# Attention and expert kernel on one core: TensorE's steps in a new order, grouped by the shape in which the array is tiled

## What is computed

```python
h = _layernorm(x) * (1 + ca) + sa
x = x + ga * attn(h)      # 16 heads of 64, 4 key/value heads, window 128, soft cap 30
h = _layernorm(x) * (1 + cb) + sb
x = x + gb * moe(h)       # 8 experts, top 1, capacity 512 tokens, relu MLP 128-512-128
# attn: scores = 30 * tanh(q.k / (8 * 30)), softmax over the last 128 tokens, times v, times Wo
```

## Time and profile before

| what | value |
| --- | --- |
| median of 3 runs | 445.53 us |
| the profiled execution, first to last instruction | 445.2 us |
| mean granted TensorE clock, share of full | 0.984 |
| TensorE busy | 425.6 us (96%) |
| VectorE, ScalarE, GpSimd busy | 295.0, 301.1, 310.4 us |
| share of TensorE in the chain that ended last | 89% |

### The profile page before, as it was taken

How to read it: one execution, slowest core, us unless ns; L and a number is a source line. 1 busy time by engine, 2 the same in 40 slices (tenths; PEclk the granted TensorE clock), 3 DMA queues, 4 the chain that set the end, 5 groups by cost and what they waited for, 6 DMA issues and landing times.

```text
span 445.2 us, 15084 instructions
## 1 busy us (share of the span) xinstructions
PE 425.6 (96%) x5662; PEld 296.0 (66%) x5662; DVE 295.0 (66%) x884; ACT 301.1 (68%) x541; POOL 310.4 (70%) x496
## 2 busy tenths in 40 slices
PE   7989999999999999999999999999998988999992
PEld 3856666665767676667676766667674554789992
DVE  6466476866776767666868585767667666386751
ACT  4887676868786868687868687867765634555540
POOL 3545666778886878687878776777687784266563
PEclk8899999999999999999999999999999998999998
DMA  8654702010111111011112210212121044595110
GB/s 240 215 175 161 215 3 84 27 32 22 52 39 38 33 55 58 20 47 52 57 41 72 64 33 20 77 40 61 37 69 43 27 143 125 186 367 198 35 44 28
DMA packets 33023, 37.15 MB, mean 83 GB/s; under 512 B 3650, under 2 KB 29255, under 8 KB 32952
## 3 DMA queue, kind: packets, MB, share of 16 engines
q1 hardware_dynamic: 29448, 27.43, 19.9%
q0 software_dynamic: 3072, 8.37, 5.2%
q10 hardware_dynamic: 432, 0.40, 0.4%
HBM read 15.69 MB, written 16.91 MB: 73 GB/s over the span
## 4 chain that ended last, share of the span: by engine, by line
PE 89%; DVE 4%; issue 2%; POOL 2%; DMA 1%; ACT 1%; POOLq 0%; SPq 0%; DVEq 0%; ACTq 0%
PE turns L504 13%; PE own L468 8%; PE turns L392 8%; PE turns L524 7%; PE turns L511 6%; PE turns L472 6%; PE turns L798 6%; PE turns L394 6%; PE turns L393 6%; PE turns L538 4%; PE turns L543 3%; PE turns L539 3%; PE own L461 2%; PE own L736 2%; PE turns L550 1%
## 5 line engine op out<-in xcount | busy, mean ns | idle before, releaser
L1189 DVE COPY_PREDICATED own<-before,turns 128x1024 f32<-128x1024 uint32 x56 | 68.8, 1228 | 41.7 <-PE turns L472 41.7
L1707 POOL TENSOR_TENSOR OL<-O,OH 128x512 fp32r<-128x512 f32 x64 | 81.7, 1284 | 16.3 <-ACT OH L923 16.2
L910 ACT ACTIVATE PR<-own 128x1024 f32<-128x1024 f32 x64 | 65.4, 1022 | 15.6 <-DVE own L1189 15.6
L1698 POOL TENSOR_SCALAR_AFFINE_SELECT PM<-PR 128x1024 f32<-128x1024 f32 x64 | 70.2, 1098 | 7.4 <-ACT PR L916 7.1
L916 ACT ACTIVATE PR<-PR 128x1024 f32<-128x1024 f32 x64 | 67.2, 1050 | 0.1
L468 PE MATMUL own<-Q,K 64*32 64x128 f32 (+3 forms) x896 | 58.7, 441 | 2.8 <-issue 1.4
L472 PE MATMUL turns<-Q,K 64*32 64x128 f32 (+3 forms) x896 | 57.4, 429 | 0.0
L1222 DVE TENSOR_TENSOR O<-turns,R 128x512 f32<-128x512 f32 x64 | 43.0, 682 | 18.3 <-PE turns L511 18.2
L1752 POOL DMA_INDIRECT sorted_rows<-PAY,slot_i x32 | 34.6, 1080 | 14.9 <-issue 10.7
L472 PEld LDWEIGHTS turns<-Q,K 64*32 64x32 f32 x896 | 36.6, 107 | 9.5
L896 ACT ACTIVATE Q<-turns 128x512 f32<-128x512 f32 x64 | 38.3, 600 | 6.6 <-PE turns L394 5.4
(11 more groups left out here) (207 smaller groups left out, 1065.8 us busy)
## 6 DMA issues: line engine op xcount, KB each, us to landing
sorted_rows<-empty_row SPq DMA_DIRECT2D x8, 776.0 KB, 6.0
VM<-V SPq DMA_DIRECT2D x56, 64.0 KB, 2.1
out_dram<-PAY SPq DMA_DIRECT2D x32, 64.0 KB, 2.4
w_stage<-w_dram SPq DMA_DIRECT2D x8, 256.0 KB
PR<-sorted_rows SPq DMA_DIRECT2D x2, 776.0 KB, 9.3
x_sb<-sorted_rows SPq DMA_DIRECT2D x2, 776.0 KB, 11.6
x_sb<-x_dram SPq DMA_DIRECT2D x3, 512.0 KB, 5.8
O<-w_dram SPq DMA_DIRECT2D x4, 256.0 KB, 4.0
```

The costliest lines, as they stand in the source:

```text
L910: act.activation(pr, own[:, :, :].rearrange("p a n -> p (a n)"), ACT.Tanh, scale=SCORE_SCALE).then_inc(tanhed, 1)
L1189: dve.copy_predicated(own[:, :, :].rearrange("p a (r n) -> p (a r) n", n=P), before[:, :].bitcast(U32).unsqueeze(1).to_broadcast([P, 2 * R ...
L1698: pool.affine_select(out=PM[:, u % P_RING, :].rearrange("p (r n) -> p r n", n=P), in_=PR[:, u % P_RING, :].rearrange("p (r n) -> p r n", n ...
L1707: pool.tensor_tensor(OL[:, t % 2, :, half], O[:, t % 2, :, half], OH[:, t % 2, :, half].bitcast(F32), ALU.subtract).then_inc(ol_done, 1)
```

## The change

The work of TensorE is the same 391 steps. What changes:

- The order. `sums(t)` now stands right before `attend(t)` (both begin at 128*32), and the first half of the next score right after it (corrections and scores are both 64*32). The projections of a block stand together. The same count gives 160 changes of form: 52 from the whole array to a tiled form, 52 back, 56 between tiled forms; 22 of them lie before `score(4, 1)` and 18 from `score(30, 0)` on. 25 times a 128*32 step follows another, 23 times a 64*32 step another; before, this happened once.
- In `attend`, the waits for the masked probabilities and for VD move from its head to its corrections.
- New banks for nearly every step, with a longer table of exceptions for the first and last tiles.
- New orders on ScalarE, VectorE and GpSimd, with longer prologues and epilogues written out. The order of SyncE is the same, and so is all from the expert stage on.

```diff
 OF_TILES = ("before", "pv", "sums", "y", "h2", "logits", "count")
 HOME = {
-    ("idle",): 5, ("columns",): 4, ("rows",): 2,
-    ("before", 0, 0): 3, ("before", 0, 1): 1, ("before", 1, 0): 0, ("before", 1, 1): 3,
-    ("count", 0): 2, ("count", 1): 0,
-    ("h2", 0): 2, ("h2", 1): 1,
-    ("k",): 1,
-    ("logits", 0): 3, ("logits", 1): 2,
-    ("pv", 0): 1, ("pv", 1): 3,
-    ("q", 0): 3, ("q", 1): 5, ("q", 2): 5, ("q", 3): 2,
-    ("sums", 0): 1, ("sums", 1): 5,
-    ("v",): 4,
-    ("wo",): 4,
-    ("x",): 0,
-    ("y", 0): 0, ("y", 1): 5,
+    ("columns",): 4,
+    ("idle",): 5,
+    ("rows",): 2,
+    ("before", 0, 0): 0, ("before", 0, 1): 0, ("before", 1, 0): 1, ("before", 1, 1): 0,
+    ("count", 0): 4, ("count", 1): 4,
+    ("h2", 0): 4, ("h2", 1): 4,
+    ("k",): 2,
+    ("logits", 0): 2, ("logits", 1): 4,
+    ("pv", 0): 2, ("pv", 1): 4,
+    ("q", 0): 5, ("q", 1): 1, ("q", 2): 0, ("q", 3): 5,
+    ("sums", 0): 5, ("sums", 1): 2,
+    ("v",): 3,
+    ("wo",): 3,
+    ("x",): 2,
+    ("y", 0): 3, ("y", 1): 5,
 }
 
-LAST_HOME = {("logits", LAST): 4, ("count", LAST - 1): 5}
+
+HOME_AT_ENDS = {
+    ("before", 1, 0): 0, ("before", LAST - 2, 0): 0, ("before", LAST - 2, 1): 3,
+    ("count", 0): 0, ("count", LAST - 3): 1,
+    ("h2", LAST - 5): 0,
+    ("k", BLOCKS - 1): 5,
+    ("logits", LAST - 5): 0, ("logits", LAST - 4): 0, ("logits", LAST): 2,
+    ("pv", 0): 4,
+    ("q", 0, 3): 4, ("q", 1, 0): 4, ("q", 1, 2): 5, ("q", 1, 3): 2, ("q", 2, 3): 3,
+    ("q", BLOCKS - 1, 0): 2,
+    ("sums", 0): 2, ("sums", 1): 3, ("sums", 2): 4, ("sums", LAST - 3): 4, ("sums", LAST - 1): 2,
+    ("v", BLOCKS - 1): 0,
+    ("wo", BLOCKS - 3): 0, ("wo", BLOCKS - 2): 0, ("wo", BLOCKS - 1): 0,
+    ("x", 0): 0, ("x", 2): 3, ("x", BLOCKS - 2): 1,
+    ("y", LAST - 2): 1,
+}
...
             def take(*use):
                 n = HOME[use[0], *(use[1] % 2, *use[2:])] if use[0] in OF_TILES else HOME[use[0], *use[2:]]
-                n = LAST_HOME.get(use, n)
+                n = HOME_AT_ENDS.get(use, n)
...
-                pe.wait_ge(masked, 2 * t + 2)
                 if t % 2 == 0:
                     pe.wait_ge(v_kept, t // 2 + 1)
-                if not first(t):
+                if first(t):
+                    pe.wait_ge(masked, 2 * t + 2)
+                else:
                     pe.wait_ge(exped, 2 * t + 2)
-                    pe.wait_ge(vd_done, later_tiles(t) + 1)
                     pe.wait_ge(mixed_in[t % VM_RING], 32 * mixes(t))
...
                 if not first(t):
+                    pe.wait_ge(masked, 2 * t + 2)
+                    pe.wait_ge(vd_done, later_tiles(t) + 1)
                     for x in range(2):
...
+            for e in range(-8, TILES - 18, 2):
+                if is_tile(e + 4):
+                    count(e + 4)
+                if is_tile(e + 12):
+                    score(e + 12, 1)
+                if is_tile(e + 8):
+                    turn_y(e + 8)
+                if is_tile(e + 5):
+                    count(e + 5)
+                if is_tile(e + 11):
+                    sums(e + 11)
+                    attend(e + 11)
+                if is_tile(e + 13):
+                    score(e + 13, 0)
+                if is_tile(e + 14):
+                    project_q(e // 2 + 7, 2)
+                    project_q(e // 2 + 7, 3)
+                if is_tile(e + 7):
+                    turn_h2(e + 7)
+                if is_tile(e + 14):
+                    project_v(e // 2 + 7)
+                    project_q(e // 2 + 7, 1)
+                    project_q(e // 2 + 7, 0)
+                    project_k(e // 2 + 7)
+                if is_tile(e + 7):
+                    score_experts(e + 7)
+                if is_tile(e + 13):
+                    score(e + 13, 1)
+                if is_tile(e + 12):
+                    sums(e + 12)
+                    attend(e + 12)
+                if is_tile(e + 14):
+                    score(e + 14, 0)
+                if is_tile(e + 9):
+                    turn_y(e + 9)
+                if is_tile(e + 8):
+                    turn_h2(e + 8)
+                if is_tile(e + 18):
+                    turn_x(e // 2 + 9)
+                if is_tile(e + 10):
+                    out_project(e // 2 + 5)
+                if is_tile(e + 8):
+                    score_experts(e + 8)
...
```

More of the change, by code:

```diff
@@ L618, in program_pe @@
             project_q(1, 2)
-            score(1, 0)
-            for e in range(-10, TILES - 14, 2):
-                if is_tile(e + 12):
[L625 to L629, removed]
+            project_v(1)
+            sums(0)
+            score(1, 1)
+            attend(0)
+            turn_x(3)
+            score(2, 0)
+            sums(1)
@@ L1376, in program_dve @@
                 if is_tile(e - 6):
[L1377 to L1379 removed]
+                    locate(e - 6)
                 if is_tile(e - 5):
[L1381 to L1390 removed]
@@ L1449, in program_dve @@
[L1449 to L1464 removed]
+                    which(e - 5)
+                if is_tile(e - 4):
+                    keep_logits(e - 4)
@@ new lines, in program_dve @@
+                if is_tile(e - 3):
+                    normalise2(e - 3)
+                    modulate2(e - 3)
+                    shift2(e - 3)
+            add_x(LAST - 11)
+            invert_gate(LAST - 14)
+            locate(LAST - 14)
+            top8(LAST - 13)
+            measure2(LAST - 11)
+            turn_sums(LAST - 8)
+            gather2(LAST - 11)
+            invert(LAST - 8)
+            spread(LAST - 8)
+            normalise2(LAST - 11)
+            which(LAST - 13)
+            modulate2(LAST - 11)
@@ new lines, in program_dve @@
+            gather2(LAST - 10)
+            negate(LAST - 13)
+            low_x(BLOCKS - 1)
+            normalise2(LAST - 10)
+            locate(LAST - 13)
+            keep_logits(LAST - 11)
+            top8(LAST - 11)
+            which(LAST - 12)
+            invert_gate(LAST - 13)
+            negate(LAST - 12)
+            modulate2(LAST - 10)
+            shift2(LAST - 10)
+            which(LAST - 11)
+            add_x(LAST - 9)
+            locate(LAST - 12)
+            merge(LAST - 5, 1)
@@ new lines, in program_dve @@
+            top8(LAST - 10)
+            invert(LAST - 5)
+            spread(LAST - 5)
+            which(LAST - 10)
+            scale(LAST - 5, 0)
+            scale(LAST - 5, 1)
+            add_x(LAST - 8)
+            negate(LAST - 10)
+            merge(LAST - 3, 0)
+            measure2(LAST - 8)
+            gather2(LAST - 8)
+            normalise2(LAST - 8)
+            modulate2(LAST - 8)
+            invert_gate(LAST - 11)
+            keep_logits(LAST - 9)
+            shift2(LAST - 8)
@@ new lines, in program_dve @@
+            invert_gate(LAST - 10)
+            locate(LAST - 11)
+            add_x(LAST - 7)
+            locate(LAST - 10)
+            top8(LAST - 9)
+            merge(LAST - 3, 1)
+            measure2(LAST - 7)
+            negate(LAST - 9)
+            which(LAST - 9)
+            turn_sums(LAST - 4)
+            invert(LAST - 4)
+            spread(LAST - 4)
+            gather2(LAST - 7)
+            invert_gate(LAST - 9)
+            scale(LAST - 4, 0)
+            scale(LAST - 4, 1)
@@ new lines, in program_pool @@
+            scatter(LAST - 13)
+            number_slot(LAST - 12)
+            rstd2_of(LAST - 8)
+            mark(LAST - 10)
+            add_seen(LAST - 10)
+            mask(LAST - 4, 1)
+            name_row(LAST - 8)
+            low_o(LAST - 5, 0)
+            scatter(LAST - 12)
+            differ(LAST - 2)
+            name_row(LAST - 7)
+            mask(LAST - 3, 0)
+            name_row(LAST - 6)
+            number_slot(LAST - 11)
+            rstd2_of(LAST - 7)
+            mark(LAST - 9)
```

927 lines of the change are left out of this document (577 added, 350 removed).

## The result

The changed kernel takes 441.98 us (median of 4 runs, 441.13 to 443.52) beside 445.57 us for the kernel before (4 runs); the ratio is 0.9927 [0.9907, 0.9948]. Run again in another session, five rounds, it was 441.85 beside 445.67, ratio 0.9927 [0.9914, 0.994]. So the gain is 3.6 to 3.8 us, and the forecast was 10.

A forecast was written before the change was run, and what follows sets the result against it. TensorE's own stream was taken to set the pace through mid-attention. 445.2 - 14.9 (form changes) + 4.6 (new waits) + 0.3 (one more change in the tail) = 435.2, with the median 0.3 above: 435.5 us, range 430 to 442.5.

The forecast's parts named there:

- The price of a change of form: TensorE's stream: 0.35 us per trip between tiled and whole array, 0.13 between tiled forms; 14.9 us saved in all.
- The rival at 0.04: TensorE's joins: two steps of one form standing together gain nothing, taking 6.2 us back, 441.7 us; chance 0.04.
- The new waits in mid-stream: Attention loop: the faster TensorE stream waits for other engines, 0.35 us a pass, 4.6 over 13 passes, bounds 0 and 8.
- project_q(.,3): Attention loop: this projection waits 0.2 to 0.4 us for its bank, which VectorE's scale frees; taken as 0.35.
- The prologue: Start of the kernel: a new wait at score(2,1) cancels the old 1.4 us at score(1,0); net 0, bounds -1 and +2.
- The stream's end: End of attention on TensorE: earlier by the 14.9 us of saved form changes less 4.6 of new waits.
- the tail: Router and norm chains after attention: same instructions on the other engines, so change 0, bounds -2 and +2 us.
- a longer stretch at the lower clock: Start of the expert stage: listed as a sign of a wrong forecast; twice the low-clock stretch would cost 1.6 us.
- Rival (4): End of the kernel: what is saved in mid-stream is waited for in the tail, leaving 445.5 us; chance 0.07.
- The edit of attend's waits: Attend: waits for mask and VD moved to the corrections; mask done long before in both orders, so costed at nothing.
- Rival (3): Attention loop: late GpSimd delays VectorE's scale, then projections; slower from 1.15 us a pass, 451.4 at 1.6; chance 0.08.
- Rival (2): Attention loop: evacuating engines set the pace, GpSimd at 21.6 us a pass or banks 0.8 late; 440.3 us; chance 0.12.

The follow-up runs named there:

- sums_apart: Changed kernel with one whole-array step (count or score_experts) put between sums and attend, twice a pass, same work: 450.38 us, ratio to before 1.0103.
- less_gpsimd: Changed kernel with GpSimd computing only 8 of VD's 256 columns from tile 5 on (old differences in later corrections): 438.52 us, ratio to before 0.9846.
- tail_even_fill: Changed kernel with all zero matmuls of the tail spread over the gaps, one of 128 or 512 columns at most places: 440.27 us, ratio to before 0.9912.
- tail_fill_gap: Changed kernel with two more zero-matmul calls, one on either side of turn_h2(LAST - 2): 440.95 us, ratio to before 0.9913.
- warm_and_even: Changed kernel with wider zero matmuls in the prologue and those of the tail spread around every router step: ratio to before 0.9923; repeated, 439.18 us, 0.9862.
- tail_no_fill: Changed kernel without the three zero-matmul calls ahead of turn_h2(30): 440.79 us, ratio to before 0.9907.
- tail_bare: Changed kernel without any of the five zero-matmul calls behind count(LAST - 3): 441.75 us, ratio to before 0.9917.
- warm_start: Changed kernel with the first zero matmuls of the prologue four times as wide: 440.35 us, ratio to before 0.9896.
- before_warm: Kernel before with the first zero matmuls of the prologue four times as wide: ratio to before 0.9981.

## Why the forecast came out as it did

**The price of a change of form** was right: 0.13 for a join of two 128*32 steps, 0.15 of two 64*32 steps, and 0.40 a trip in sums_apart where the rows gave 0.35. That each change has a price agrees with the Trainium skill (TensorEngine Tiling (Array Packing), Key Properties: changing the tiling mode drains TensorE), which gives no figure for it. The rival at 0.04, that two steps of one form gain nothing by standing together, is ruled out by both joins. The rule that I had set beside it (the Trainium skill, TensorE: Matmul & The Clock Gate, What overlaps and what doesn't: a weight load overlaps running matmuls only where the row group differs) has no run here that tests it by itself; the joins gained all the same.

**The new waits in mid-stream** were undersized and put in the wrong place. A regular pass without waits is 20.83 us; the one shown took 21.45, so 0.62 of waits and not 0.35. Over nine passes, score(7,1) to score(25,1), the gain is 9.9 - 5.2 = 4.7 us. The orders as written have 58 changes fewer there, worth 10.0 us at the forecast's prices. So the waits took 5.3, or 0.58 a pass, just inside the bound of 0.6. project_q(.,3), where I put the wait, does not wait in the pass shown. 0.30 a pass was GpSimd's (less_gpsimd), which I had found to fit with 0.2 us to spare: `low_o` ahead of the last matmuls of out_project. The rest is small waits for banks at turn_x, turn_y, project_k and count, read off the timeline as excess between starts and not tested one by one. Most of them the view of waits doesn't show.

**The prologue** was forecast at 0. Its waits did not cancel. From score(0,0) to score(7,1) the new order has 19 changes fewer (3.4 us) and puts off the seven steps (1.6 us by the estimate above), which would make 5.0 us; the gain there is 5.15 - 1.84 = 3.3. So about 1.7 us went into waits beyond those of the old prologue, inside the bound of 2. They are the waits at score(2,0), sums(1) and score(2,1) listed above: I had walked only the last of these. The 1.8 us that stand at score(0,0) already are the other way. 1.1 of them are there when the first projection starts (8.98 instead of 10.07), and most of the rest is the clock's earlier rise. Both differ as much between executions of one order, so this part is luck of the two profiled executions, and not shown as a gain of the new order.

**The stream's end** came out nearly right for the wrong reasons: 9.5 us early where 14.9 - 4.6 = 10.3 was forecast. Without the 1.8 us of the start it is 7.6 or 7.7, so the waits took about 7.2 us and not 4.6: 5.3 in the nine passes, 1.7 in the prologue, some tenths behind. With that the sum comes close to the medians: 14.9 - 7.2 - 3.7 (the tail, below) = 4.0 us, and 3.6 were measured.

**The step that failed is the tail**: "I take 0 and bound it by -2 and +2". It was +3.7 us. I reasoned that the chains of the other engines are the same instructions and follow the last attend, and that two turn_h2 stand behind more. I did not walk TensorE's order there. The walk would have shown the eight small steps from turn_h2(28) to count(28) in a row, waiting for other engines with no zero matmuls between, and then three calls of these in a block ahead of a step that the chain needs. I also looked for the clock only in the first 4 us of the expert stage, where it fell before; with the new order the fall came 9.1 us behind the first corrections of tile 31 instead of 15.7, in the middle of the chain. I named the sign ("a longer stretch at the lower clock") but gave it no term. The new waits above were undersized too, but stayed inside their bounds; the tail did not. Rival (4), that what is saved in mid-stream is waited for in the tail, had 0.07; it held for more than a third of the saving, and my argument against it (the chains start when the last attend ends) is true, but the chains run through TensorE's own queue.

**The edit of attend's waits** was costed at nothing because the mask is done long before. In steady state it is. At attend(26) it is not, behind a scatter that came late, and there the edit is worth 1.7 to 2 us. It belongs to the new order: with the waits at the head, the interval of the ratio leaves a gain of 0 to 2 us only.

**The other rivals.** Rival (3), which needed 1.15 us a pass, did not come. No experiment took work from ScalarE or VectorE, so that they are no bound is not shown: the waits that less_gpsimd leaves, 0.28 us a pass, may be theirs. Rival (2) saw GpSimd at work, rightly, but put the pass at 21.6; the one shown has 21.45. The band of rival (2), 440 to 443.3, holds the measured 441.98, but its mechanism holds only in part: GpSimd took 0.30 us a pass, and the loss in the tail is none of it.

What stays open: which banks' waits make up the remaining 0.28 us a pass, and why the clock rises up to 4 us sooner in the prologue of some executions than of others.

## What to carry to other kernels

A stream that gets denser in its steady part saves only what its end lets through: walk the end step by step on every engine as carefully as the loop, the filler instructions included. Here a filler was paid in full where its successor was ready, and double at the lower clock; a small one in each gap did better than a block in one. And read the pace from start to start against the length that a step has undisturbed, since a wait inside a group of matmuls isn't listed as one.

## What the runs showed of the chip

- The clock fell at 356.8 us in after, while TensorE stood for the second of three waits of 1.01, 0.96 and 0.51 us with short steps between them, and came back at about 370.5, after the placing of rows had begun at 1.2 GHz. In the seven other profiled kernels that leave this gap open it fell too, 0.4 to 3.0 us behind the start of turn_h2(29). In the four profiles with zero matmuls in the gap it fell at 360.1 (tail_even_fill), at 365.4 (tail_fill_gap) or not at all (warm_and_even and its repeat). The Trainium skill (TensorE: Matmul & The Clock Gate, Why this matters for your kernels) warns of single long pauses; here it was a row of short ones, and the measurement decides.
- Taking zero matmuls out shortened the stretch by 2.1 us where they held up a ready step (tail_no_fill), and taking out the others as well lengthened it again by 1.0 (tail_bare), in one profile each.
- The start of score(0,0) differs by 1.8 us between nine profiled kernels with the same prologue, and in them the clock rises between 10.3 and 14.6 us. In the three with wide zero matmuls (warm_start, warm_and_even and its repeat) it rises between 10.3 and 11.7 us, and score(0,0) starts between 14.58 and 15.03.
- A session can be slower in one stage: in the one where the kernel before took 453.7 us, before_warm reached score(31,1) at 346.82, as before did, and its first expert matmul at 380.08 (before 380.82); from there to the end it took 70.6 us, and before 64.4.
